# The front of an attention and spiking feed-forward kernel: two buffer sets for high and low parts, x issued by ACT, the first stack in two pieces, the first maxima in blocks 5 to 7

## What is computed

```
q, k, v = split(xn @ w_qkv);  q, k = irfft(rfft(.) * sigmoid(mask_logits))   per head, 16 heads of 16
a = softmax(q k^T / 4) v, all heads;  out_a = a @ w_out + b_out
h = relu(xn @ W_fc^T)^2;  y = h @ W_proj^T;  five leaky integrate-and-fire steps on y; mean of spikes
out = x + out_a + spikes
```

## Time and profile before

| | us |
|---|---|
| median of 3 runs (1845.75 to 1850.59) | 1849.54 |
| the profiled execution | 1849.1 |
| its span | 1847.3 |
| PE busy | 1816.0 (98%) |
| DVE busy | 1423.0 (77%) |
| ACT busy | 1074.7 (58%) |
| POOL busy | 711.7 (39%) |

### The profile page before, as it was taken

The page is one execution under the profiler, slowest core; times in us unless marked ns, Lnnn a source line. Parts: engine busy times, 40 slices in busy tenths (PEclk is TensorE's granted clock), DMA queues, the critical chain, the costliest instruction groups (busy, mean ns, idle before and its releaser), DMA issues.

```text
span 1847.3 us, 35475 instructions
## 1 busy us (share of the span) xinstructions
PE 1816.0 (98%) x14288; PEld 1091.7 (59%) x14288; DVE 1423.0 (77%) x1781; ACT 1074.7 (58%) x1181; POOL 711.7 (39%) x948
## 2 busy tenths in 40 slices
PE   6889999999999999999999999999999999999998
PEld 4555666555555656555566665555566565555666
DVE  5576778777877788778877787778777877788765
ACT  3325666666666666666666666666666666666662
POOL 1000444433334444433344444333344443333445
PEclk9998999999999999999999999999999999999999
DMA  4752222211222222201222222112222222112223
GB/s 155 221 201 42 44 44 40 42 32 23 42 44 43 44 44 38 43 20 34 44 43 44 44 39 43 30 23 44 44 43 44 44 39 42 20 36 44 43 84 106
DMA packets 85950, 98.81 MB, mean 53 GB/s; under 512 B 50774, under 2 KB 64854, under 8 KB 81690
## 3 DMA queue, kind: packets, MB, share of 16 engines
q1 hardware_dynamic: 85788, 96.56, 23.9%
HBM read 70.80 MB, written 20.99 MB: 50 GB/s over the span
## 4 chain that ended last, share of the span: by engine, by line
PE 94%; DMA 2%; SPq 2%; DVE 1%; issue 0%; ACT 0%; ACTq 0%; DVEq 0%
PE ring L632 31%; PE banks L642 28%; PE ring L622 18%; PE banks L699 6%; PE banks L704 6%; PE ring L783 2%; PE banks L571 1%; SPq L247 1%; PE ring L624 1%; DMA qk_scratch<-hid_sb 1%; DMA attnT<-x 1%; DVE pmax L844 1%; PE ring L562 0%; DMA counts<-wv 0%; PE ring L583 0%
## 5 line engine op out<-in xcount | busy, mean ns | idle before, releaser
L850 DVE TENSOR_REDUCE pmax<-ring 128x2 f32<-128x1024 f32 x1000 | 1176.8, 1218 | 329.0 <-PE ring L624 326.3
L501 ACT ACTIVATE probs<-ring 128x1024 f32<-128x1024 f32 x1024 | 993.4, 1022 | 635.9 <-PE ring L632 635.9
L632 PE MATMUL ring<-qst,kst 66*128 66x512 f32 x2048 | 615.0, 422 | 0.0
L642 PE MATMUL banks<-probs,vst 128*32 128x256 f32 x8192 | 548.7, 385 | 0.1
L632 PEld LDWEIGHTS ring<-qst,kst 66*128 66x128 f32 x2048 | 345.3, 188 | 257.7 <-issue 209.2
L622 PE MATMUL ring<-kst,qst 64*128 64x512 f32 x1000 | 387.8, 467 | 0.0
L624 PE MATMUL ring<-kup,qup 64*128 64x512 f32 x1000 | 387.3, 467 | 0.0
L642 PEld LDWEIGHTS banks<-probs,vst 128*32 128x32 f32 x8192 | 213.8, 109 | 213.7 <-issue 125.1
L421 POOL TENSOR_TENSOR lif<-lif 128x256 f32<-128x256 f32 x32 | 21.7, 677 | 793.3 <-ACT y_sb L517 793.3
L622 PEld LDWEIGHTS ring<-kst,qst 64*128 64x128 f32 x1000 | 183.2, 184 | 159.1 <-DVE pmax L850 82.2
L624 PEld LDWEIGHTS ring<-kup,qup 64*128 64x128 f32 x1000 | 183.1, 183 | 0.0
(11 more groups left out here) (71 smaller groups left out, 681.9 us busy)
## 6 DMA issues: line engine op xcount, KB each, us to landing
qst<-qk_scratch SPq DMA_DIRECT2D x128, 128.0 KB, 4.1
kst<-qk_scratch SPq DMA_DIRECT2D x64, 256.0 KB, 5.9
qup<-qk_scratch SPq DMA_DIRECT2D x252, 64.0 KB, 4.5
qk_scratch<-probs SPq DMA_DIRECT2D x32, 256.0 KB
kup<-qk_scratch SPq DMA_DIRECT2D x64, 128.0 KB, 6.4
attnT<-x SPq DMA_DIRECT2D x8, 512.0 KB, 7.6
qk_scratch<-relu_sb SPq DMA_DIRECT2D x16, 256.0 KB
qk_scratch<-hid_sb SPq DMA_DIRECT2D x16, 256.0 KB
```

The lines of the kernel that those rows point to most:

```text
L501: act.activation(probs[:, s % PS, :], score_slot(g), ACT.Exp, scale=SCALE).then_inc(exp_done, 1)
L632: mm = pe.matmul(score_slot(g)[:, c * BLK:(c + 1) * BLK], kst[b][:, kt * P:(kt + 1) * P], qst[b][:, q:q + BLK], start=True, stop=True)
L642: mm = pe.matmul(po[32 * j:32 * (j + 1), half * D:(half + 1) * D], vst[b][:, kt, :], quarters[:, j], start=(kt == 0), stop=(kt == TB - 1))
L850: dve.tensor_reduce(pmax[:, tile, first:first + 2], unit_slot(g).rearrange("p (c e) -> p c e", c=2), AX, ALU.max).then_inc(mx_taken, 1)
```

## The change

The Fori loops over blocks 0 to 3 are written out. High and low parts have two sets of buffers, for even and odd blocks (the second lies in attnT), each with a semaphore of its own, so `take_high` of block t waits for the stores of block t - 2. x of blocks 2 to 7 is issued by ACT, as `load_x(t + 3)` behind `take_transposed(t + 1)`. The first stack comes in two pieces of 1024 tokens, after the stores of block 2 and of block 4; `first_part` gives the maxima an order that needs only piece 0 for the first 16. Blocks 5, 6 and 7 have 16 first maxima each and none are left behind block 7. Blocks 6 and 7 are both normalised in block 4, block 6 in three parts between the low parts. The table of Exp is loaded in block 4. `store_shift(0, 0, 0)` is issued ahead of the stores of block 7; wproj, wout and bout are loaded after them. PE waits for single weights later, and ACT for the stores whose buffers it reuses.

```diff
@@ buffers for high and low parts
-        hilo = [t.rearrange("p (c t) -> p c t", c=2) for t in
-                (probs[:, 2, :], probs[:, 3, :], relu_sb[:, :, :].rearrange("p f t -> p (f t)"),
-                 hid_sb[:, :, :].rearrange("p f t -> p (f t)"))]
+        hilo = [[t.rearrange("p (c t) -> p c t", c=2) for t in
+                 (probs[:, 2, :], probs[:, 3, :], relu_sb[:, :, :].rearrange("p f t -> p (f t)"),
+                  hid_sb[:, :, :].rearrange("p f t -> p (f t)"))],
+                [attnT[:, 1, w * HALF:(w + 1) * HALF].rearrange("p (c t) -> p c t", c=2) for w in range(QB)]]
+        def first_part(n):
+            if n < 2 * TB:
+                return n % TB // 2, n // TB * 2 + n % 2
+            return n // 4, n % 4
@@ SP
+            def load_first(piece):
+                for w in range(QB):
+                    for k in range(2):
+                        sp.wait_ge(stored[w][k], 32 * (piece + 1))
+                cols = slice(piece * HALF, (piece + 1) * HALF)
...
-            for t in range(NB // 2, NB):
-                if t < NB - 2:
-                    next_x(t, t % 2)
-                if t == NB // 2:
-                    for w in range(QB):
-                        sp.wait_ge(stored[w], 32 * (NB // 2 + 1))
-                    sp.wait_ge(zero_out, 64)
-                    load_stack(0, 0)
-                    sp.dma_start(qst[0][4 * DH:ROWS, :].bitcast(F32), zero_dram).then_inc(blank_in, 16)
+            for t in range(NB):
+                store_block(t)
+                if t == 2:
+                    sp.wait_ge(zero_out, 64)
+                    sp.dma_start(qst[0][4 * DH:ROWS, :].bitcast(F32), zero_dram).then_inc(blank_in, 16)
+                    load_first(0)
+                if t == 4:
+                    load_first(1)
+                if t == 5:
+                    sp.dma_start(wfc_sb[:], wfc.rearrange("(c p) e -> p c e", p=P)).then_inc(wfc_in, 16)
                     load_upper_keys(0, 0)
                     load_upper_queries(0, 0, 1)
-                store_block(t)
...
-            store_shift(0, 0, 0)
+                if t == NB - 2:
+                    store_shift(0, 0, 0)
+            sp.dma_start(wproj_sb[:], wproj.rearrange("(c p) e -> p c e", p=P)).then_inc(wproj_in, 16)
+            sp.dma_start(wout_sb[:], wout.rearrange("(c p) e -> p c e", p=P)).then_inc(late_in, 16)
+            sp.dma_start(bout_sb[:], bout.partition_broadcast(P)).then_inc(late_in, 16)
             for w in range(QB):
-                sp.wait_ge(stored[w], 32 * (NB + 1))
+                for k in range(2):
+                    sp.wait_ge(stored[w][k], 32 * (NB // 2))
@@ ACT
+            def load_x(t):
+                act.wait_ge(ln_done, t - 1)
+                act.dma_start(x_in[:, t % 2], x_blocks[t]).then_inc(x_landed[t % 2], 16)
+            def take_high(t, w):
+                act.wait_ge(qk_ready, QB * t + w + 1)
+                if t > 1:
+                    act.wait_ge(stored[w][t % 2], 32 * (t // 2))
+                act.activation(hilo[t % 2][w][:, 0, :].bitcast(F32R), qk_psum(w), ACT.Copy).then_inc(hi_ready, 1)
...
+            load_x(2)
+            for t in range(NB):
+                for w in range(QB):
+                    take_high(t, w)
+                    if t == 4 and w == 1:
+                        deviation(6)
                 if t < NB - 1:
                     take_transposed(t + 1, (t + 1) % 2)
-                if t < NB - 2:
+                if t < NB - 3:
+                    load_x(t + 3)
+                if t < 4:
                     deviation(t + 2)
+                if t == 4:
+                    deviation(7)
+                    act.activation(filt[:, 1, 0:1], filt[:, 0, 0:1], ACT.Exp)
                 take_v(t)
...
             for s in range(FIRST):
+                if s in (2, 3):
+                    act.wait_ge(stored[s - 2][0], 32 * (NB // 2))
@@ PE
+            for t in range(NB):
+                project_qk(t, t % 2, TB * (t - 5) if t > 4 else None)
                 if t < NB - 1:
                     next_transpose(t + 1, (t + 1) % 2)
-                project_v(t, t % 2, chunk + 2 * QB if units > QB else None)
-                chunk += 2 * units
+                project_v(t, t % 2, TB * (t - 5) + 8 if t > 4 else None)
...
-            for n in range(chunk, 2 * (UNITS - LEAD)):
-                first_max(n)
@@ DVE
+            for t in range(NB):
+                for w in range(QB):
+                    if t > 4:
+                        for n in range(2):
+                            first_max(TB * (t - 5) + 2 * w + n)
+                    low_part(t, w)
+                    if t == 4 and w < 3:
+                        (block_stats, block_rstd, block_scale)[w](6)
+                if t < 4:
+                    normalise(t + 2)
+                if t == 4:
+                    normalise(7)
                 if t == NB - 1:
                     for link in range(4):
                         split_shift(link, 0, 0, 2 * TB)
-                if units > QB:
-                    for n in range(chunk + 2 * QB, chunk + 2 * units):
-                        first_max(n)
-                chunk += 2 * units
-            for n in range(chunk, 2 * (UNITS - LEAD)):
-                first_max(n)
+                if t > 4:
+                    for n in range(8):
+                        first_max(TB * (t - 5) + 8 + n)
```

More of the change, by code:

```diff
@@ L42 @@
 QK_BANKS = 2
-AHEAD = [0, 4, 8, 8]
+PIECE = 6 * 16
 USES = 3
@@ L167, in build @@
         lo_done = sem("lo_done")
-        stored = [sem(f"stored{i}") for i in range(QB)]
+        stored = [[sem(f"stored{i}_{k}") for k in range(2)] for i in range(QB)]
         v_ready = sem("v_ready")
         v_taken = sem("v_taken")
+        first_in = [sem(f"first_in{i}") for i in range(2)]
         stack_in = [sem(f"stack_in{i}") for i in range(2)]
@@ L291, in move_output @@
                     sp.dma_start(dst[:, :, j, :], src).then_inc(out_moved[b][half], 16)
[L293 to L300, removed]
-            for t in range(NB // 2, NB):
-                if t < NB - 2:
-                    next_x(t, t % 2)
-                if t == NB // 2:
-                    for w in range(QB):
-                        sp.wait_ge(stored[w], 32 * (NB // 2 + 1))
+            def load_first(piece):
[3 more added lines that the diff above has]
+                cols = slice(piece * HALF, (piece + 1) * HALF)
+                for part in range(2):
+                    for dup in range(2):
+                        r = (2 * part + dup) * DH
+                        sp.dma_start(qst[0][r:r + DH, cols].bitcast(F32), qk_dram[0, 0, part, :, cols]).then_inc(first_in[piece], 16)
+                for dup in range(2):
+                    r = dup * 2 * DH
+                    sp.dma_start(kst[0][r:r + 2 * DH, cols].bitcast(F32),
+                                 qk_dram[1, 0, :, :, cols].rearrange("r d t -> (r d) t")).then_inc(first_in[piece], 16)
@@ L523, in _ @@
             act.wait_ge(xnt_copied, NB + 2)
-            for w in range(QB):
-                act.wait_ge(stored[w], 32 * (NB + 1))
             for s in range(FIRST):
+                if s in (2, 3):
+                    act.wait_ge(stored[s - 2][0], 32 * (NB // 2))
                 if s == 4:
+                    for w in (2, 3):
+                        act.wait_ge(stored[w][0], 32 * (NB // 2))
                     take_up(0, 0, UP_A)
@@ L851, in unit_max, with low_part @@
                                   unit_slot(g).rearrange("p (c e) -> p c e", c=2), AX, ALU.max).then_inc(mx_taken, 1)
-            def low_parts(t, n=None):
-                for w in range(QB):
-                    if n is not None:
-                        for c in range(2):
-                            first_max(n + 2 * w + c)
-                    dve.wait_ge(hi_ready, QB * t + w + 1)
-                    dve.tensor_tensor(hilo[w][:, 1, :].bitcast(F32R), qk_psum(w), hilo[w][:, 0, :],
-                                      ALU.subtract).then_inc(lo_done, 1)
+            def low_part(t, w):
+                dve.wait_ge(hi_ready, QB * t + w + 1)
+                dve.tensor_tensor(hilo[t % 2][w][:, 1, :].bitcast(F32R), qk_psum(w), hilo[t % 2][w][:, 0, :],
+                                  ALU.subtract).then_inc(lo_done, 1)
             def split_shift(link, n, half, chunks=None):
@@ L885, in _ @@
             dve.memset(shift[:, 16:32], 0.0).then_inc(shift_blank, 1)
-            normalise(0, 0, 0)
+            normalise(0)
             build_filter()
-            normalise(1, 0, 1)
-            with dve.Fori(0, NB // 4) as n:
-                for p in range(2):
-                    t = 2 * n + p
-                    low_parts(t)
-                    normalise(t + 2, n + 1, p)
-            chunk = 0
-            for t in range(NB // 2, NB):
-                units = AHEAD[t - NB // 2]
-                low_parts(t, chunk if units else None)
-                if t < NB - 2:
-                    normalise(t + 2, t // 2 + 1, t % 2)
+            normalise(1)
```

(2 more changed lines are left out.)

85 lines of the change are left out of this document (32 added, 53 removed).

## The result

The changed kernel takes 1859.01 us, a median of 4 runs (1857.61 to 1860.7), against 1849.15 for the kernel before (4 runs). The ratio is 1.0057, with a 95% interval of 1.0046 to 1.0069: slower by 0.6%, where the prediction had 1847 and a range of 1839 to 1856.

The account below looks back on a forecast made before the run. PE, with 94% of the chain, bounds the kernel through its waits and clock. E at 125.3 plus 28.8 and 3.5 of clock loss puts s = 8 at 157.6 against 159.98: 1849.1 - 2.4 = 1846.7, so 1847, range 1839 to 1856.

Parts of the forecast that it names:

- The two waits: PE idle 5 to 6 us at block 5's third maximum, and 9 us ahead of the scores of s = 8.
- the second half's stack: Stack of batch 1, loaded between E and s = 8: 10.5 us from first issue to landed, plus 0.5 for weights.
- s = 8: Point in PE's main part, four pairs after its first scores; predicted at E + 28.8 = 154.1, against 159.98 before.
- the sum: Terms along PE's path to E, then to s = 8, with clock loss: 2.4 us saved from 1849.1, giving 1846.7.
- PE's go in block 5: PE resuming after its stop at block 5's third maximum, behind the normalising of block 7: predicted at 86.6.
- E: End of block 7's q and k projections, where its v begins: predicted 125.3, 4.0 us sooner than 129.27.
- SP's go: Moment SP goes on to the stack of batch 1, after waiting for the shift and issuing block 7's stores: E + 17.8.
- three weight loads of 1.25 MB issued between: 0.5: Weights queued between block 7's stores and batch 1's stack: 0.5 us, using the 0.47 stores leave free; 4 in series.
- the upper sum: Forecast's high end, 1852.5: E at 129.1, then 28.8 us, with 5.5 us lost to the clock.
- the rival of a DMA-bound front: Blocks 4 to 6: stores, x and pieces exceed 11.27 us a block, ACT waits; 3 us give 1850; chance 0.08.
- The rival with x late: Front: x of blocks 6 and 7 lands in 7.6 and 12.6 us, E 134.1, time 1857.5; chance 0.14.
- the 0.16: Chance of a time over 1855: 0.12 from the rival with x late and 0.04 from the others.

Follow-up runs that it names:

- the shift first, with early weights: Changed kernel with x of blocks 6 and 7 issued earlier and weights behind block 6's stores, first shift still ahead of block 7's stores: 1839.57 us, ratio 0.9952.

## Why the prediction was wrong

**The two waits were foreseen; the second half's stack was mis-sized.** The prediction named a wait at the third maximum of block 5 and one at s = 8, and they decide the result. In the sum, s = 8 was to stand at 154.1; it stands at 166.09, 12.0 us later. The terms:

| term | predicted | measured |
|---|---|---|
| x of blocks 6 and 7, issue to use | 5.7 and 5.7 | 8.5 and 8.3 |
| PE's go in block 5 | 86.6 | 90.84 |
| from there to E | 38.7 | 37.3 |
| E | 125.3 | 128.15 |
| E to SP's go for the stack | 17.8 | 19.4 |
| stack, with the weights ahead of it | 11.0 | 18.6 |
| s = 8 | 154.1 | 166.09 |
| lost at the lower clock behind it | 3.5 | 2.9 |

**The step that failed** is "three weight loads of 1.25 MB issued between: 0.5". The stack with the weights took 7.6 us more than the 11.0 of the sum: 7.0 for the weights, by the kernel that has them behind block 6's stores, instead of 0.5, and 11.6 for the stack without them instead of the 10.5 of the earlier trace rows. That is beyond both ends that I had given the weights, 0 and 4, and the upper sum, 1852.5, held only the 0.5. Later kernels point the same way: the stack took 17.0 and 17.3 us with the weights right ahead of it (x sooner; x from SP) and 11.4 without (the shift first, with early weights). The term took the share that the stores leave free. But from 142 to 144, with the first of the weights issued, the share is still 0.53; they move from 144 on, SP's go is at 147.53, and the stack leaves no free share: alone, in the kernel before, it had them at a share of 0.91 to 1.16 from 139 to 147. Why the weights cost 7.0 us there, and why the stack behind them took at most 14.2 us when the shift stood behind the stores, stays open; the small DMAs right behind the stack are one candidate.

**The rest of the 12.0 us.** E came 2.9 us late: PE's go in block 5 came 4.2 late, as x landed late both times, and PE then needed 37.3 us to E and not 38.7. That E still lies inside the 123.2 to 129.1 of the sum, with both landings over 7.6, is in part luck: in the four other kernels with this stop PE needed 38.6 to 38.9 us, and E was 129.1, 129.4, 131.8 and 138.0. From E to SP's go it took 1.6 more, for the stores: 14.4 us from their first issue to the go against 13.0 in the sum; the windows have them at 189 and 160 GB/s from 136 to 140, not at 204.

**The landing of x** was taken between idle and the median of the earlier trace rows, as if a queue of its own were half the cure. From ACT x landed in 3.7 us on idle engines and in 8.0 to 9.2 us beside stores, and with early issue it landed in the same 8 us; so what else the engines carried decided, though their share beside the stores is only 0.53. Why half-free engines bring x so late no run shows. The eight-kilobyte shift in ACT's queue took 4.8 us from its last issue.

The Trainium skill (DMA: Bandwidth & Descriptors, Queues, rings and completion order) says that an engine takes turns between the queues packet by packet. By that rule 5.7 looked near or a little high. The measurements decide: a queue of its own did not bring short waits. The first page of the Trainium skill (Trainium Kernel Development and Optimization, Key Constraints) says that issuing from several engines saves only issue time. That gave 7.6 us and E = 129.1 and was the nearer, to the landings (8.5 and 8.2) and to E (128.15).

**What held.** E + 2.23 for the shift, turned in by 130.38, DVE keeping up with 16 maxima a block, the stop at the third maximum, first scores behind E by 6.5 at the upper clock, 204 GB/s for the stores (205 at 70 to 72), and no wait of ACT for stores, so the rival of a DMA-bound front fell. The rival with x late had the sign right, but neither its landings nor its place for the loss: x took 8.5 and 8.2 us, not 7.6 and 12.6, E came 1.1 us sooner than before, and the loss lay in the tail. So the time came out slower for a reason that the 0.16 hardly held: the tail's terms for the stores, the stack and the weights all came out larger, and the upper sum gave none of them more than the middle one did.

**What the change is worth without its two waits.** The same front with x issued sooner, the shift from ACT and the weights behind the stack is 1% faster than before. So the rest of the change, taken together, gains; its parts were not tried one by one, but for the second buffer set, which was worth about nothing. What failed were three places in issue order: of x, of the first shift and of the weights.

## What to carry to other kernels

Before moving a wait ahead of DMAs on a queue's engine, follow the last of those DMAs to whoever reads its data, and count the full chain: issue, data at the rate of the row, and all that is queued between. A queue of its own doesn't make a load quick where the engines carry other data (8.0 to 9.2 us for x from ACT, 3.7 on idle engines), so start it when its buffer comes free and not where it fits the program. Time a transfer in the company it will have: 10.5 us for the stack became 11.6 with small DMAs behind it and 18.6 with 1.25 MB ahead of it too.

## What the runs showed of the hardware

- Four DMAs of 2 KB in ACT's queue let PE go on 4.8 us behind their last issue, as SP's 2.10 MB of stores ended, and 2.7 us behind it with the weights last, where the stores ended sooner.
- The issue of one 256 KB load (wout) took 0.58 us in two kernels, and 3.18, 4.86, 5.07 and 5.61 us in the four that have x sooner and the weights right behind block 6's stores.
- After a wait of 2.16 or 2.17 us PE went on at the upper clock in one execution and at the lower in another; after 3.60 at the upper for four matmuls (1.15 us) and then at the lower (1.70 us at 132.09); after 5.74 at the lower from the start. The runs of each of the two kernels with a wait of 2.16 or 2.17 us spread over 7.6 us.
- DMA engines at a share over 1 moved 119 GB/s in the changed kernel (150 to 152, the stack's loads among them) and 411 in the one with x sooner (94 to 96, behind the issues of wfc and the upper keys and queries).
